# First layer of a four-layer program: side work spread over the steps, heads divided by their sums on VectorE instead of copied by ScalarE

## The chip, the core and the metric

The program runs on one core of a Trainium2 chip. Five engines work side by side on it, each on its own list of instructions in order: TensorE (PE in the profile, with its weight loads as PEld), VectorE (DVE), ScalarE (ACT), GpSimd (POOL) and SyncE (SP), which here only issues DMAs. They wait for each other by semaphores. Matmul results land in eight PSUM banks of 128 x 512 fp32; everything else lies in SBUF. The metric is the device time of the whole program in microseconds, the median of several runs.

## The reference

Four blocks are computed one after the other on x of shape (4, 512, 512), each as x + layernorm(block(layernorm(x))). Only the first two blocks are touched here; the kernel calls them together "the first layer":

```python
x = x + _layernorm(_L0_attn_ref(_layernorm(x), Wq, Wkv, Wo))
x = x + _layernorm(_L0_ffn_ref(_layernorm(x), q_scales, q_vals, bias))
...
# _L0_attn_ref: 32 heads of width 16, one key and one value head for all
q = (h @ Wq).reshape(b, s, 32, 16)
kv = h @ Wkv
k, v = kv[..., :16], kv[..., 16:]
scores = einsum('bqhd,bkd->bhqk', q, k) * 16 ** -0.5
bias = slopes[:, None, None] * (pos[None, None, :] - pos[None, :, None])
scores = where(causal, scores + bias, -inf)
out = einsum('bhqk,bkd->bqhd', softmax(scores), v).reshape(b, s, 512)
return out @ Wo
# _L0_ffn_ref: one product with a dequantized 512 x 512 matrix, plus a bias
```

## The kernel before

The function layer0 holds the first layer. Matmuls are done in fp16 with every operand split in a high and a low part (names ending in _hi and _lo), so one product is three matmuls.

**Steps.** The 32 heads are taken in 16 pairs for each of the 4 batch elements, 64 pairs p in all. The code of every engine is one loop over steps n from -6 to 80, and what an engine does in step n is fixed by lags. In step n:

- TensorE writes five banks of scores of pair n (L598, L600), interleaved with five banks of exponents of pair n-6 (L610, L612), which ScalarE turns into weights (L814, `weights_and_hi`). These are "turns" 0 to 4: one bank of each. After turn 1 comes the product of weights and values of pair n-8 (weigh_values, L628 and L631, 60 small matmuls) into a bank called pv. Its column 16 of every 17 is the sum of the weights.
- VectorE takes the maximum of each scores bank (L976, L978, L981), and subtracts to get the low part of the weights of pair n-7 in two pieces (weights_lo, L990): one ahead of maxima 0 and 1, one ahead of maxima 2 and 3. `mx` and `mp` hold the maxima; every fourth step they are joined (L996, L998).
- GpSimd casts the weights of pair n-6 to fp16 (L533, three casts, the last one for the fifth bank alone) and does the low part of the fifth bank (L535).
- pv of pair n-8: ScalarE copies the bank to the tile `ob` (copy_heads, L821) behind its third exponential. VectorE takes reciprocals of the sums in `ob` into `ro` as nearly the last thing in the step (sum_reciprocals, L1009). GpSimd multiplies one step later (N_LAG = 9, norm_heads, L524) into `on`, named heads_normed in the profile.

**Side work.** The rest of the layer hangs in the same steps, by the tables FRONT, BACK and NORM of due steps, repeated every 16 steps for the next batch element: q (query projection, every fourth step, n = 3, 7, 11, ...), K and V, y (output projection), f (feed-forward), and transposes of rows, four for a batch element: n1 (`front_T`), o (`heads_T`), n2 (`back_T`), n3 (`xT`). others(n) lists the fills of a step. The first of them is done by TensorE around turn 3, the others between turns 3 and 4; a transpose of the maxima, m, comes in steps divisible by 4, ahead of the others but the first. VectorE evacuates the first between maximum 3 and maximum 4 and the others behind maximum 4; ScalarE does the same around its fourth and fifth exponential.

**Banks.** Scores have three banks, exponents two, and all fills of the step besides have three ("rest"), used in turn: pv, first other, m, other others. take(u) makes TensorE wait until the filling three places earlier in that list has been emptied. So a fourth filling in a step waits for the same step's pv bank. Steps with scores that have four or more: 8, 24, 25, 36, 37, 40, 41, 47, 48, 52 and 53. Without scores: 64, 68 and 69.

**Layernorms.** norms_at(n) gives the normalisations due in step n: n1, a1, n2, a2, n3. For n1, n2 and n3 VectorE takes the statistics of four tiles in one step (L907), then the variance (L915, L917); GpSimd computes the reciprocal deviation in the next step (rstd, L510 to L514); at the end of that step ScalarE normalises the four tiles (L807). For a1 and a2 GpSimd then adds the four tiles to `xb` (add_rows, L545), two at the end of one step and two at the start of the next. With scores running, statistics bursts of four stand in steps 3, 19 and 35 (n1), 33 and 49 (n2), 43 and 59 (n3); one more in step 65 (n2). After a K, ScalarE also makes four key stacks at the end of one step (stack_keys, L837).

## Time and profile before

| what | value |
|---|---|
| median of three runs | 2259.62 us (2256.56 to 2260.6) |
| profiled execution | 2258.78 us, span 2256.8 us |
| busy share | PE 92%, DVE 78%, ACT 62%, POOL 41% |
| steps 8 to 69 of the first layer | about 118 to 626 us of the span |
| second layer, from about 710 us | not touched by the change |

The span is the traced part of the execution; about 2 us lie outside. The page's busy shares are averages over stages with different limits. The stage with the change is read by stretches of the span, and within it step by step: a step starts where VectorE takes its first maximum of a pair.

### The profile page before, as it was taken

How to read it: one execution, taken by the hardware profiler on the slowest of the kernel's cores; microseconds unless marked ns; L12 is line 12 of the kernel's file. 1: busy time of each engine (PE TensorE's matmuls, PEld its weight loads, DVE VectorE, ACT ScalarE, POOL GpSimd, SP SyncE). 2: the span in 40 equal slices, each digit the busy share in tenths (PEclk: the TensorE clock that was granted, in tenths of full speed). 3: DMA queues.
4: the chain of work that ended last, by engine and by line, in shares of the span. 5: the costliest groups of instructions: out<-in, count | busy, mean ns of one | idle time of the engine just before them, and what ended most of it. 6: DMA issues, size and time to landing. Idle time of an engine off the chain costs nothing. (4 is left out here: it accounts for less than half of the span.)

```text
span 2256.8 us, 48541 instructions
## 1 busy us (share of the span) xinstructions
PE 2078.5 (92%) x18563; PEld 1258.3 (56%) x18563; DVE 1771.4 (78%) x3711; ACT 1391.5 (62%) x3037; POOL 930.4 (41%) x901
## 2 busy tenths in 40 slices
PE   8688978889767799999999999999999999988998
PEld 3366656566534456666566665656666665533443
DVE  5699898899765787877787887878878787977665
ACT  2555555555644776777777687777777777761222
POOL 0177776678934323233332323333232333353221
PEclk9899989999778999999999999999999999999999
DMA  5210100101022354444444454454344444520100
GB/s 202 78 35 17 44 20 16 46 17 46 3 80 81 71 88 89 90 71 92 85 77 90 81 100 69 81 97 90 68 90 90 71 81 80 101 75 19 38 20 38
DMA packets 390214, 153.81 MB, mean 68 GB/s; under 512 B 358544, under 2 KB 369424, under 8 KB 387936
## 3 DMA queue, kind: packets, MB, share of 16 engines
q1 hardware_dynamic: 389984, 150.71, 30.5%
q8 instruction: 148, 2.42, 0.5%
q14 instruction: 82, 0.67, 0.1%
HBM read 48.69 MB, written 11.53 MB: 27 GB/s over the span
## 5 line engine op out<-in xcount | busy, mean ns | idle before, releaser
L1762 POOL TENSOR_TENSOR q_in_sbuf<-q_in_sbuf,sinq 128x512 f32<-128x512 f32 x128 | 162.6, 1270 | 720.7 <-ACT q_in_sbuf L1894 598.1
L1906 ACT ACTIVATE xp<-xp,nm 128x128 f32<-128x128 f32 (+3 forms) x512 | 281.3, 550 | 199.1 <-DVE nm L1989 199.1
L1788 PE MATMUL bank<-xT_hi,weights_and_hi 128*128 128x512 f16 x1280 | 381.9, 380 | 6.2 <-DVE yacc L2004 3.5
L814 ACT ACTIVATE weights_and_hi<-bank,unit 128x512 f32<-128x512 f32 x320 | 212.0, 687 | 191.4 <-PE bank L612 187.7
L1871 ACT ACTIVATE probs_hi<-xp,rl 128x128 f16<-128x128 f32 (+3 forms) x512 | 245.1, 550 | 67.8 <-DVE rl L2009 64.4
L1958 DVE SCALAR_TENSOR_TENSOR probs_lo<-xp,rl,probs_hi 128x128 f16<-128x128 f32 (+3 forms) x512 | 282.2, 611 | 0.0
L1966 DVE TENSOR_TENSOR q1T_lo<-qf,q1T_hi 128x512 f16<-128x512 f32 x128 | 88.4, 690 | 223.3 <-ACT q1T_hi L1885 223.3
L1989 DVE CUSTOM_DVE_ANT_0 xp<-bank,mask,cs 128x128 f32<-128x128 f32 (+3 forms) x512 | 250.1, 544 | 0.0
L1788 PE MATMUL bank<-xT_lo,weights_and_hi 128*128 128x512 f16 x640 | 243.0, 380 | 0.0
L533 POOL CAST weights_and_hi<-weights_and_hi 128x1024 f16<-128x1024 f32 (+1 forms) x192 | 188.6, 995 | 116.7 <-ACT weights_and_hi L814 116.5
L1788 PE MATMUL bank<-p1T_hi,v_hi 128*128 128x128 f16 x1280 | 223.1, 220 | 3.3 <-DMA p1T_lo<-probs_lo 3.3
L1788 PE MATMUL bank<-p1T_hi,v_lo 128*128 128x128 f16 x1280 | 223.0, 220 | 0.0
L1788 PE MATMUL bank<-p1T_lo,v_hi 128*128 128x128 f16 x1280 | 222.9, 220 | 0.0
L1788 PEld LDWEIGHTS bank<-xT_hi,weights_and_hi 128*128 128x128 f16 x1280 | 124.3, 98 | 159.7 <-issue 13.5
L1769 POOL TENSOR_TENSOR qf<-q_in_sbuf,t 128x512 f32<-128x512 f32 x160 | 203.8, 1274 | 12.7 <-POOL q_in_sbuf L1762 0.2
L1788 PE MATMUL bank<-wo_hi,o1T_hi 128*128 128x512 f16 x512 | 194.8, 380 | 6.3 <-DVE wo_lo L2048 4.7
L1788 PE MATMUL bank<-wo_hi,o1T_lo 128*128 128x512 f16 x512 | 194.7, 380 | 0.0
L1788 PE MATMUL bank<-wo_lo,o1T_hi 128*128 128x512 f16 x512 | 194.6, 380 | 0.0
L598 PE MATMUL bank<-k_stack_max,q_stack 128*128 128x512 f16 (+3 forms) x512 | 139.9, 316 | 51.7 <-DVE mx L976 35.7
L990 DVE TENSOR_TENSOR weights_lo<-weights_and_hi 128x1024 f16<-128x1024 f32 x128 | 180.4, 1414 | 3.9 <-POOL weights_and_hi L533 3.9
L610 PE MATMUL bank<-q_stack,k_stack 128*128 128x512 f16 (+3 forms) x512 | 143.4, 321 | 23.3 <-ACT weights_and_hi L814 20.7
L1788 PE MATMUL bank<-kT_hi,q1T_hi 128*128 128x128 f16 (+3 forms) x512 | 147.0, 300 | 11.0 <-DVE q1T_lo L1966 7.2
(307 smaller groups left out, 5510.5 us busy)
## 6 DMA issues: line engine op xcount, KB each, us to landing
weights_and_hi<-in_wq SPq DMA_DIRECT2D x8, 1024.0 KB, 5.6
raw_o<-in_wo SPq DMA_DIRECT2D x8, 1024.0 KB, 5.8
x_front<-in_x SPq DMA_DIRECT2D x4, 1024.0 KB, 6.6
q_stack<-q_hi SPq DMA_DIRECT2D x64, 64.0 KB, 2.6
xb<-in_x SPq DMA_DIRECT2D x4, 1024.0 KB, 5.5
wup<-in_wup SPq DMA_DIRECT2D x3, 1024.0 KB, 12.1
fused_scratch<-weights_and_hi SPq DMA_DIRECT2D x12, 256.0 KB, 3.0
x_scratch<-xb SPq DMA_DIRECT2D x3, 1024.0 KB, 4.3
```

What stands on the lines that cost most here:

```text
L533: pool.tensor_copy(ph[0][:, p % 2, c0:c1, :], px[:, p % 2, c0:c1, :]).then_inc(s_wh, 1)
L598: pe.matmul(out[:, c:c + w], qs[:, g % GP, pp, t * P:(t + 1) * P], kz[:, g // GP % 2, e, 0:w], start=True, stop=False)
L610: pe.matmul(out[:, c:c + S - j * P], ks[:, g // GP % 2, e, j * P:(j + 1) * P], qs[:, g % GP, pp, j * P:S], start=True, stop=False)
L814: act.activation(px[:, p % 2, i, :], bank_of(("x", p, i))[:, :], ACT.Exp, scale=unit[:, 0:1]).then_inc(s_ed, 1)
L990: dve.tensor_tensor(ph[1][:, p % 2, c, :], px[:, p % 2, c, :], ph[0][:, p % 2, c, :], ALU.subtract).then_inc(s_wl, 1)
L1762: pool.tensor_tensor(qs[:, i % 2, :], qs[:, i % 2, :], rope["sink" if u[0] == "k" else "sinq"][:, :], ALU.mult).then_inc(s_rot, 1)
L1769: pool.tensor_tensor(qf[:, i % 2, :], qs[:, i % 2, :], t2[:, i % 2, :], ALU.add).then_inc(s_qf, 1)
L1788: ins = pe.matmul(out, lhs(a), rhs(c), start=(first and i == 0), stop=(last and i == 2))
L1871: ins = act.activation(pr[0][:, m % 2, c], xp[:, m % 3, c], ACT.Copy, scale=rl[:, m % 3, t:t + 1])
L1906: ins = act.activation(x, x, ACT.Exp, scale=-1.0, bias=nm[:, m % 3, t:t + 1], accum_out=ls[:, m % 3, t:t + 1])
L1958: ins = dve.scalar_tensor_tensor(pr[1][:, m % 2, c], xp[:, m % 3, c], rl[:, m % 3, t:t + 1], pr[0][:, m % 2, c], ALU.mult, ALU.subtract)
L1989: ins = dve.tensor_tensor_reduce(out=xp[:, m % 3, TRI[t]:TRI[t] + w], in0=bank_of(("s", m, i))[:, col:col + w], in1=mask[:, S - w:S], scal ...
```

## The change

**Heads.** copy_heads, the tile `ob` and the semaphore s_pv_out are gone. VectorE takes the reciprocals straight from the pv bank, behind maximum 3 of the same step, then evacuates the first other fill, and then multiplies from the bank into `on`. The multiplication's semaphore, s_heads_normed, now tells TensorE that the pv bank is empty. GpSimd's norm_heads is gone.

**Side work.** The four statistics of n1 go to four steps (the last in the step of the variance, three steps later than before), those of n2 and n3 to two steps, two in each, with the variance one step later. One of a step's statistics stands ahead of the multiplication, the others behind maximum 4. ScalarE normalises two tiles behind its exponentials 3 and 4 of a step, and two behind exponentials 0 and 1 of the next, instead of four at the end. The key stacks are dealt out in the same way, and VectorE's last key operation moves one step later. GpSimd's four additions stand one at the end of a step, one at the start and one at the end of the next, and one at the start of the third. The store of x2 comes one step later.

```diff
-        X_LAG, V_LAG, N_LAG = 6, 8, 9
+        X_LAG, V_LAG = 6, 8
...
-        NORM = {"n1": -13, "a1": 30, "n2": 33, "a2": 40, "n3": 43}
+        NORM = {"n1": -10, "a1": 30, "n2": 34, "a2": 40, "n3": 44}
+        STATS = {"n1": (-13, -12, -11, -10), "n2": (33, 33, 34, 34), "n3": (43, 43, 44, 44)}
...
-        signals = {"s": (s_sf, s_sd), "x": (s_ef, s_ed), "pv": (s_pf, s_pd), ...
+        signals = {"s": (s_sf, s_sd), "x": (s_ef, s_ed), "pv": (s_pf, s_on), ...
...
 # GpSimd
                 for n in STEPS:
-                    for u in norms_at(n - 3):
-                        if u in add_no:
-                            add_rows(u, (2, 3))
+                    adds_at(n - 4, 3)
+                    adds_at(n - 3, 1)
                     for u in norms_at(n - 1):
                         rstd(norm_no[u])
-                    if 0 <= n - N_LAG < NP:
-                        norm_heads(n - N_LAG)
                     if 0 <= n - X_LAG < NP:
                         weights_hi(n - X_LAG)
-                    for u in norms_at(n - 2):
-                        if u in add_no:
-                            add_rows(u, (0, 1))
+                    adds_at(n - 3, 2)
+                    adds_at(n - 2, 0)
...
 # ScalarE
-                        if i == 2 and 0 <= n - V_LAG < NP:
-                            copy_heads(n - V_LAG)
...
-                    b = at(n, FRONT["K"] + 1)
-                    if b is not None:
-                        stack_keys(b)
-                    for u in norms_at(n - 1):
-                        normalise(u)
+                        for u in norms_at(n - 2) if i < 2 else norms_at(n - 1) if i > 2 else ():
+                            normalise(u, i + 2 if i < 2 else i - 3)
+                        if i > 2 and at(n, FRONT["K"] + 1) is not None:
+                            stack_keys(at(n, FRONT["K"] + 1), 0, i - 3)
+                        if i < 2 and at(n, FRONT["K"] + 2) is not None:
+                            stack_keys(at(n, FRONT["K"] + 2), 1, i)
...
 # VectorE
+                def pv_out(p):
+                    return bank_of(("pv", p))[:, 0:2 * TT * EV].rearrange("p (e t c) -> p e t c", e=2, c=EV)
+
                 def sum_reciprocals(p):
-                    dve.wait_ge(*emptied[("pv", p)])
-                    if p >= 3:
-                        dve.wait_ge(s_on, p - 2)
-                    dve.reciprocal(ro[:, p % 3, :, :], ob[:, p % 3, :, :, E0]).then_inc(s_ro, 1)
+                    dve.wait_ge(*filled[("pv", p)])
+                    dve.reciprocal(ro[:, p % 2, :, :], pv_out(p)[:, :, :, E0]).then_inc(s_ro, 1)
+
+                def norm_heads(p):
+                    b, c = p // PAIRS, 2 * (p % PAIRS) * E0
+                    if p % GP == 0 and b >= 1:
+                        dve.wait_ge(*filled[("o", b - 1, p % PAIRS // GP)])
+                    dve.wait_ge(s_ro, p + 1)
+                    o = pv_out(p)
+                    dve.tensor_tensor(on[:, :, c:c + 2 * E0].rearrange("p t (e c) -> p e t c", e=2),
+                                      o[:, :, :, 0:E0], ro[:, p % 2, :, :].unsqueeze(3).to_broadcast([P, 2, TT, E0]),
+                                      ALU.mult).then_inc(s_on, 1)
...
                     if 0 <= n < NP:
                         maximise(n, (2, 3))
+                    if 0 <= n - V_LAG < NP:
+                        sum_reciprocals(n - V_LAG)
                     for u in extra[:1]:
                         evacuate(u)
+                    if at(n, FRONT["K"] + 1) is not None:
+                        add_key_maxima(at(n, FRONT["K"] + 1))
+                    some_statistics(stats_at(n)[:1])
+                    if 0 <= n - V_LAG < NP:
+                        norm_heads(n - V_LAG)
                     if 0 <= n < NP:
                         maximise(n, (4,))
...
                     for u in extra[1:]:
                         evacuate(u)
+                    some_statistics(stats_at(n)[1:])
                     for u in norms_at(n):
-                        kind, b = u
...
                         variance(u)
-                    if 0 <= n - V_LAG < NP:
-                        sum_reciprocals(n - V_LAG)
```

VectorE around step 19, whose n1 statistics are dealt out. First the kernel before:

```order
L978 TENSOR_REDUCE mp<-bank 128x4 x2
L953 SCALAR_TENSOR_TENSOR q_lo<-bank,fq,q_hi 128x512
L981 TENSOR_REDUCE mx<-bank 128x2
L907 BN_STATS st<-x_front 128x6 x4
L915 BN_AGGR mv<-st 128x2 x4
L917 TENSOR_SCALAR ve<-mv 128x4
L1009 RECIPROCAL ro<-ob 128x8
L996 TENSOR_REDUCE mx<-mp 128x8
L998 COPY mx<-mp 128x8
L990 TENSOR_TENSOR weights_lo<-weights_and_hi 128x1024
```

The same place in the change, down to the second statistics in step 20:

```order
L964 TENSOR_REDUCE mp<-bank 128x4 x2
L996 RECIPROCAL ro<-bank 128x8
L939 SCALAR_TENSOR_TENSOR q_lo<-bank,fq,q_hi 128x512
L891 BN_STATS st<-x_front 128x6
L1004 TENSOR_TENSOR heads_normed<-bank,ro 128x2x4x16
L967 TENSOR_REDUCE mx<-bank 128x2
L982 TENSOR_REDUCE mx<-mp 128x8
L984 COPY mx<-mp 128x8
L976 TENSOR_TENSOR weights_lo<-weights_and_hi 128x1024
L962 TENSOR_REDUCE mx<-bank 128x1 x2
L976 TENSOR_TENSOR weights_lo<-weights_and_hi 128x1024
L964 TENSOR_REDUCE mp<-bank 128x4 x2
```

One statistics instruction and the multiplication stand where four statistics and the variance did; the reciprocal has gone up, from the end of the step to behind maximum 3.

VectorE in step 24, which has two transposes besides m. First before:

```order
L990 TENSOR_TENSOR weights_lo<-weights_and_hi 128x1024
L978 TENSOR_REDUCE mp<-bank 128x4 x2
L921 TENSOR_TENSOR front_T_lo<-bank,front_T_hi 128x4x128
L981 TENSOR_REDUCE mx<-bank 128x2
L1002 SCALAR_TENSOR_TENSOR m_lo<-bank,m_hi 32x128
L921 TENSOR_TENSOR front_T_lo<-bank,front_T_hi 128x4x128
L1009 RECIPROCAL ro<-ob 128x8
L990 TENSOR_TENSOR weights_lo<-weights_and_hi 128x1024
```

And in the change:

```order
L976 TENSOR_TENSOR weights_lo<-weights_and_hi 128x1024
L964 TENSOR_REDUCE mp<-bank 128x4 x2
L996 RECIPROCAL ro<-bank 128x8
L905 TENSOR_TENSOR front_T_lo<-bank,front_T_hi 128x4x128
L1004 TENSOR_TENSOR heads_normed<-bank,ro 128x2x4x16
L967 TENSOR_REDUCE mx<-bank 128x2
L988 SCALAR_TENSOR_TENSOR m_lo<-bank,m_hi 32x128
L905 TENSOR_TENSOR front_T_lo<-bank,front_T_hi 128x4x128
L976 TENSOR_TENSOR weights_lo<-weights_and_hi 128x1024
```

The bank of pv is now emptied by L1004, behind maximum 3 and the first transpose's low part.

TensorE in step 24, between turns 3 and 4, with its waits. First before:

```order
L639 MATMUL bank<-ident,mx 128x128 [waits s_maxima,s_queries_out]
L645 MATMUL bank<-ident,x_front 128x128 [waits s_pv_out,s_rows_normed]
L645 MATMUL bank<-ident,x_front 128x128 x3
L598 MATMUL bank<-k_stack_max,q_stack 128x256 [waits s_scores_maximised]
L600 MATMUL bank<-tri,far 128x128
```

And in the change:

```order
L633 MATMUL bank<-ident,mx 128x128 [waits s_maxima,s_queries_out]
L639 MATMUL bank<-ident,x_front 128x128 [waits s_heads_normed,s_rows_normed]
L639 MATMUL bank<-ident,x_front 128x128 x3
L592 MATMUL bank<-k_stack_max,q_stack 128x256 [waits s_scores_maximised]
L594 MATMUL bank<-tri,far 128x128
```

TensorE's list is the same; its second transpose of the step waits for VectorE's multiplication where it waited for ScalarE's copy.

## Rows read from the trace of the kernel before

**Rows 1.** The page: busy time of each engine.

```profile
PE 2078.5 (92%) x18563; PEld 1258.3 (56%) x18563; DVE 1771.4 (78%) x3711; ACT 1391.5 (62%) x3037; POOL 930.4 (41%) x901
```

**Rows 2.** Stretches: length, busy us (instructions) by engine, granted clock, DMA share, GB/s.

```profile
118.00:626.00 508.00, 439.12 (x6413) 306.85 (x6414) 451.54 (x703) 294.61 (x523) 381.80 (x366) 0.93 0.08 27
183.50:189.70 6.20, 4.97 (x94) 3.71 (x93) 6.20 (x10) 3.51 (x6) 5.08 (x6) 1.00 0.18 58
196.00:206.10 10.10, 7.55 (x108) 4.97 (x105) 9.27 (x22) 5.01 (x9) 5.40 (x7) 0.98 0.01 2
224.80:232.90 8.10, 8.07 (x113) 5.47 (x110) 7.43 (x13) 4.45 (x8) 7.32 (x7) 1.00 0.01 3
252.80:264.00 11.20, 11.17 (x135) 6.96 (x132) 7.50 (x13) 4.96 (x9) 7.30 (x7) 1.00 0.01 4
304.30:315.80 11.50, 6.49 (x126) 4.97 (x122) 10.29 (x18) 4.16 (x8) 11.34 (x11) 0.96 0.12 37
395.00:409.00 14.00, 12.14 (x140) 7.22 (x136) 11.03 (x23) 5.52 (x10) 12.26 (x12) 1.00 0.21 76
585.20:626.00 40.80, 32.20 (x500) 22.76 (x497) 31.12 (x36) 22.28 (x40) 37.88 (x34) 0.72 0.01 2
```

**Rows 3.** Waits from 118 to 626 us: who for whom, us, times, longest.

```profile
PE bank L598 <- DVE mx L976: 32.3, 21, 4.8
PE bank L610 <- ACT weights_and_hi L814: 20.7, 21, 3.2
```

**Rows 4.** Timeline of VectorE near 302 us: start, length, instruction.

```profile
302.08 0.23 DVE L948 TENSOR_TENSOR v<-bank,v 128x64 f16<-128x64 f32 x1 [0.29 <-ACT v L782]
302.23 0.68 DVE L981 TENSOR_REDUCE mx<-bank 128x2 f32<-128x512 f32 x1
```

**Rows 5.** Timeline of VectorE at the end of step 17.

```profile
187.59 0.19 DVE L1009 RECIPROCAL ro<-ob 128x8 f32<-128x8 f32 x1
187.70 2.04 DVE L990 TENSOR_TENSOR weights_lo<-weights_and_hi 128x1024 f16<-128x1024 f32 x1
```

**Rows 6.** Timeline of GpSimd at the same time.

```profile
187.50 1.16 POOL L535 TENSOR_TENSOR weights_lo<-weights_and_hi 128x512 f16<-128x512 f32 x1
188.62 1.39 POOL L524 TENSOR_TENSOR heads_normed<-ob,ro 128x128 f32<-128x128 f32 x1
```

**Rows 7.** VectorE, groups by form from 118 to 626 us: count, busy, mean ns.

```profile
L990 DVE TENSOR_TENSOR weights_lo<-weights_and_hi 128x1024 f16<-128x1024 f32 x125 | 175.6, 1409 | 3.9 <-POOL weights_and_hi L533 3.9
```

**Rows 8.** The same by its tile: count, shortest, median and longest ns.

```profile
L990 DVE TENSOR_TENSOR weights_lo<-weights_and_hi x125: 1165/1211/2311, 119.1 to 623.6; 128x1024 f16<-128x1024 f32 x125
```

**Rows 9.** Timeline of TensorE in step 24, behind turn 3.

```profile
234.35 0.60 PE L645 MATMUL bank<-ident,x_front 128*128 128x128 f32 x4
234.78 0.27 PE L598 MATMUL bank<-k_stack_max,q_stack 128*128 128x256 f16 x1
```

**Rows 10.** Timeline of VectorE in step 24.

```profile
235.16 1.27 DVE L978 TENSOR_REDUCE mp<-bank 128x4 f32<-128x512 f32 x2
236.36 0.67 DVE L921 TENSOR_TENSOR front_T_lo<-bank,front_T_hi 128x512 f16<-128x512 f32 x1
236.96 0.68 DVE L981 TENSOR_REDUCE mx<-bank 128x2 f32<-128x512 f32 x1
```

**Rows 11.** Timeline of VectorE in step 19.

```profile
201.49 2.46 DVE L907 BATCH_NORM_STATS2 st<-x_front 128x6 f32<-128x512 f32 x4
204.06 0.38 DVE L915 BATCH_NORM_AGGREGATE mv<-st 128x2 f32<-128x6 f32 x4
```

**Rows 12.** ScalarE, groups by form from 118 to 626 us.

```profile
L821 ACT ACTIVATE ob<-bank 128x136 f32<-128x136 f32 x63 | 17.4, 276 | 0.0
```

**Rows 13.** Timeline of VectorE: low part of the queries in steps 23 and 47.

```profile
229.15 0.75 DVE L953 SCALAR_TENSOR_TENSOR q_lo<-bank,fq,q_hi 128x512 f16<-128x512 f32 x1 [0.63 <-ACT q_hi L790]
...
443.33 0.75 DVE L953 SCALAR_TENSOR_TENSOR q_lo<-bank,fq,q_hi 128x512 f16<-128x512 f32 x1 [2.02 <-ACT q_hi L790]
```

**Rows 14.** GpSimd, groups by form from 585.2 to 626 us.

```profile
L524 POOL TENSOR_TENSOR heads_normed<-ob,ro 128x128 f32<-128x128 f32 x6 | 4.2, 708 | 0.1
```

More of the change, by code:

```diff
@@ L407, in norms_at, with stats_at @@
             return out
+        def stats_at(n):
+            return [(kind, b, t) for kind in STATS for t in range(TT)
+                    for b in (at(n, STATS[kind][t]),) if b is not None and has(kind, b)]
         norms = [u for n in STEPS for u in norms_at(n)]
@@ L482, in _ @@
                         stack_queries(g)
-                    b = at(n, NORM["a2"] + 3)
+                    b = at(n, NORM["a2"] + 4)
                     if b is not None and b < LAST:
@@ L805, in normalise @@
                         act.wait_ge(s_ad, TT * (add_no["a" + str(int(kind[1]) - 1), b] + 1))
-                    for t in range(TT):
-                        act.activation(dst[:, t, :], src[:, t, :], ACT.Identity, scale=rs[:, t:t + 1],
-                                       bias=nb[:, t:t + 1]).then_inc(s_nm, 1)
+                    act.activation(dst[:, t, :], src[:, t, :], ACT.Identity, scale=rs[:, t:t + 1],
+                                   bias=nb[:, t:t + 1]).then_inc(s_nm, 1)
                 def exponential(p, i):
@@ L829, in maxima_hi, with stack_keys @@
                                    scale=-1.0 / MAXU).then_inc(s_mh, 1)
-                def stack_keys(b):
-                    for i, k in enumerate((kz, ks)):
-                        act.wait_ge(s_kb, 2 * b + i + 1)
-                        if b >= 2:
-                            act.wait_ge(*filled[("x", PAIRS * (b - 1) - 1, 4)])
-                        for e, half in enumerate(("even", "odd")):
-                            act.activation(k[:, b % 2, e, :], kb[:, i, :], ACT.Copy,
-                                           scale=row[half][:, 0:1]).then_inc(s_kr, 1)
+                def stack_keys(b, i, e):
+                    k, half = (kz, ks)[i], ("even", "odd")[e]
+                    act.wait_ge(s_kb, 2 * b + i + 1)
+                    if b >= 2:
+                        act.wait_ge(*filled[("x", PAIRS * (b - 1) - 1, 4)])
+                    act.activation(k[:, b % 2, e, :], kb[:, i, :], ACT.Copy,
+                                   scale=row[half][:, 0:1]).then_inc(s_kr, 1)
                 for n in STEPS:
@@ L936, in join_keys, with add_key_maxima @@
                                              ALU.mult, ALU.add).then_inc(s_kb, 1)
+                def add_key_maxima(b):
                     dve.wait_ge(s_kb, 2 * b + 1)
@@ L1031, in _ @@
                         evacuate(u)
+                    some_statistics(stats_at(n)[1:])
                     for u in norms_at(n):
-                        kind, b = u
-                        if kind == "n1":
-                            dve.wait_ge(s_xf, 16 * b)
-                        for t in range(TT):
-                            if kind == "n1":
-                                statistics(t, xf)
-                            elif kind in ("n2", "n3"):
-                                dve.wait_ge(s_ad, TT * add_no["a" + str(int(kind[1]) - 1), b] + t + 1)
-                                statistics(t, xb)
                         variance(u)
-                    if 0 <= n - V_LAG < NP:
-                        sum_reciprocals(n - V_LAG)
                     if n == NP + V_LAG + 2:
```

37 lines of the change are left out of this document (15 added, 22 removed).

## The prediction

> **What bounds the kernel now.** I read the page first, for the shares of the whole program [rows 1], then the stretches of the first layer, then single steps. TensorE's 92% of the page says little here: the change lies between 118 and 626 us, and in that stretch VectorE is busy 451.5 of 508 us, TensorE 439.1, GpSimd 381.8 and ScalarE 294.6 [rows 2]. VectorE and TensorE are so close that each step decides for itself. Step 17 is an ordinary one, with nothing on the side: 6.2 us, VectorE busy for all of it, TensorE for 4.97. Step 23 has a q fill: 8.1 us, TensorE busy for 8.07, VectorE for 7.43. Step 27 with q and y is TensorE's alone: 11.2 us against VectorE's 7.5. TensorE can't run far ahead, since the scores have three banks for five fills a step, and can't catch up later what it lost. So a step costs about the larger of the two engines' loads in it, plus what they spend waiting for each other. In the waits of the stretch TensorE stands 32.3 us for VectorE's maxima and 20.7 us for ScalarE's exponentials [rows 3]: the first come behind bursts of VectorE's side work, the second behind bursts of ScalarE's. These two are what dealing out can win. The time before and after the stretch has no instruction that changes much, and I take it as it is.
>
> **1. The multiplication on VectorE.** 64 instructions of 128 x 128 out of PSUM are added. No row has this form. A 128 x 64 one of the same kind holds VectorE for 0.15 us (302.08 to 302.23) [rows 4]; a 128 x 512 one for 0.60 us (236.36 to 236.96) [rows 10]. Between them, by elements, lies 0.15 + 64/448 x 0.45 = 0.21 us; that is an estimate, and 0.15 and 0.60 are its bounds. I take 0.2, near the smaller, since 128 elements are 64 from the one and 384 from the other. The reciprocal held the engine for only 0.11 us though it lasts 0.19 [rows 5]; the multiplication needs its result, so in steps without a fill between the two another 0.1 us is lost. Together some 0.3 us a step, 19 us over 64 steps (at the bounds 15 and 45). But not all of it moves the end. At the end of step 17 VectorE's weights_lo starts at 187.70 and takes 2.04 us, where the shortest takes 1.165 [rows 8], and GpSimd's L535 of 187.50 to 188.66 explains it: VectorE got on when GpSimd was through [rows 5, 6]. What delays VectorE by 0.3 us there only shortens this hold. L990 means 1409 ns over 125 instructions [rows 7], 0.24 above the shortest [rows 8], so the holds sum to 0.24 x 125 = 30 us; I find the first piece, or the small copy ahead of it, held by over 0.2 us in 36 of the 64 steps. Of the 28 others eight have the bank wait of point 2, which counts its own 0.3. That leaves 20 x 0.3 = **+6 us**. That the new instruction is held itself by GpSimd I exclude: the low parts that read a bank, like L921, take 0.67 us each time [rows 10].
>
> **2. The pv bank comes free late.** ScalarE emptied it behind its third exponential; now VectorE does, behind maximum 3 and the evacuation of the first fill. In steps with four fills TensorE needs that very bank for the fourth. In step 24 it did so at 234.35 [rows 9]. VectorE finishes maximum 3 about 236.36 and the first low part at 236.96 [rows 10]; with reciprocal and multiplication it is 237.3. TensorE stands for 3 us with turn 4 queued behind the transposes. Then four transposes (0.43 us to the next matmul [rows 9], and the scores' bank 0.35 us after that) fill the bank for maximum 4 at about 238.2, which VectorE could have taken at 237.3: 1 us idle, and maximum 4 comes 1.2 us later than before. ScalarE's fifth exponential and, behind it, the high part of the second transpose come later too, for which VectorE then waits a second time, 0.9 us; and GpSimd's L535, released by that exponential, now meets weights_lo, 0.5 us. Sum 2.6 us for step 24. Steps 8, 36 and 52 have the same pattern: 4 x 2.6 = 10. In steps 25 and 41 the fourth fill is the last: 2 x 2.2 = 4. In steps 37, 40, 47, 48 and 53 TensorE comes late by itself, with a projection or V ahead, and I take 1 us each, for the part that VectorE still needs from its evacuation to the multiplication: 5. Together **+19 us**; from both sides 5 (if only the wait for maximum 4 counts and half of it is made good in the next step) to 40 (if each costs 3.5).
>
> **3. Statistics dealt out.** Step 19 (q and a burst) takes 10.1 us where step 23 (q) takes 8.1; step 33 takes 11.5 where an ordinary one takes 6.2; step 43 (q, y) 14.0 where step 27 takes 11.2 [rows 2]: bursts cost 2.0, 5.3 and 2.8 us, 3.4 in the mean. VectorE's own work in one is 4 x 0.6 + 0.4 + 0.2 = 3.0 us [rows 11], and it stays. So a full step's filling gains only 0.4 us a burst; it was not the size of the burst but VectorE's load that was paid. To that comes that single statistics in ordinary steps go partly into the holds of point 1, I take 1.2 us a burst. Eight bursts: 8 x 1.6 = **-13 us**; between -3 and -25, the latter if all 3.0 are hidden. TensorE's idle time behind a burst isn't a gain by itself: VectorE was working.
>
> **4. ScalarE.** The 64 copies of 276 ns [rows 12] lay in time when it waited for TensorE: 0 by themselves, as ScalarE has 3.51 us of work in a 6.2 us step [rows 2]. The bursts of four normalisations and four key stacks are another matter: exponentials 0 and 1 of the next step come late, TensorE waits for them (20.7 us [rows 3]), and VectorE then waits in the q step behind, 2.02 us in step 47 against 0.63 in step 23 [rows 13]. Two of four now stand ahead of exponential 4 or behind it, where they delay the cast and L535. I count half: **-10 us**, between 0 and -20. What is late next is exponential 4.
>
> **5. GpSimd.** Its multiplication goes. In ordinary steps it lay behind weights_lo and ahead of a cast that had time (188.62) [rows 6]: 0. From 585.2 on GpSimd is busy 37.9 of 40.8 us [rows 2], and there the six that go take 4.2 us [rows 14]: **-4 us**. But GpSimd no longer waits there for VectorE's reciprocal, and in its place a cast of the next pair can start just ahead of weights_lo, which is then held as in [rows 5]. By when exponential 1, L535 and weights_lo come in each step, 14 steps are exposed, to 0.5 to 0.76 us; half of it is **+4 us**. The Trainium skill (SBUF — State Buffer, section Who interferes with whom) says that a VectorE instruction with two SBUF inputs and a GpSimd instruction that reads SBUF exclude each other, and whoever starts first keeps the ports for its whole length; the trace's 2.04 us agrees, and by that rule the full 8 to 11 us are paid, the third rival below.
>
> The queues: on SP only the store of x2 moves, by one step, and the load of the next xb behind it waits for a later normalisation, two steps ahead of its first use. Cost 0; if it were late, GpSimd's additions would wait.
>
> **Sum:** 6 + 19 - 13 - 10 - 4 + 4 = +2 us against the profiled execution of 2258.8 us; with rounding of the terms, and since the median of the runs is 0.8 us above that execution, I say 2262 us.
>
> **The rivals.**
> - *The bank wait is hidden and the spreading works.* TensorE has 1.2 us of slack in an ordinary step, and VectorE's delays might be swallowed by the holds. Then point 2 is 5, the others as above, or point 3 at -20: 6 + 5 - 16 - 12 - 4 + 4 = -17, 2243 us. For it: the 30 us of holds. Against: the fourth fill and turn 4 stand in one queue. Chance 0.32.
> - *The bank wait weighs double (the slower side).* The granted clock was 0.93 in the mean of the stretch and 0.72 from 585.2 on, where TensorE is busy for 32.2 of 40.8 us [rows 2]: where it stands more, the chip grants less. Eleven new stalls of 3 us can bring more of the lower level, 1.2 GHz, and a step with one costs 3.5 us instead of 1 to 2.6 where TensorE is needed. From 30 us for the eleven steps on it decides: 6 + 36 - 13 - 10 - 4 + 4 = +19, 2279 us. Chance 0.2.
> - *GpSimd's cast gets ahead of VectorE in all exposed steps*: 8 to 11 us instead of 4, and in the steps of point 2 as well: +9, 2269 us. Chance 0.1.
> - *It doesn't deal out as it says*: no. The order of instructions shows each move.
>
> **How the numbers follow.** The sum as it stands, 2262 us with 2256 to 2268, has 0.38, of which 0.25 lie within 0.2% of before (4.5 us, about what a measurement can tell) and 0.13 above. Faster by over 0.2%: 0.32 from the first rival. Slower: 0.13 + 0.2 + 0.1 = 0.43. The range from 2238 to 2282 leaves out a tenth at either side.
>
> **What would show it.** In the trace of the changed kernel: L1004 near 280 ns, 64 times, and weights_lo's mean below or above 1409 ns (point 1 or the third rival). In step 24 TensorE idle for about 3 us ahead of the transpose L639, released by heads_normed, and VectorE idle ahead of maximum 4 (point 2): a sum of waits of TensorE for heads_normed near 20 to 30 us; under 10 would be the first rival. VectorE's waits for q_hi near 0.65 each (point 4). TensorE's waits for ScalarE down from 20.7 us by half. The clock in the stretch at 0.93 or above, against 0.90 or lower for the second rival. The whole is wrong if the stretch of 508 us moves by over 20 us either way.

## The result and the profile after

The changed kernel takes 2284.6 us (median, 2278.3 to 2287.5) against 2259.7 for the kernel before: a ratio of 1.0109, with a 95% interval of 1.0086 to 1.0132. It is slower by about 25 us. The forecast was 2262 us, with a range up to 2282. Slower was the likeliest of the three outcomes, at 0.43, but the size lies outside the range.

The page of the kernel after: the span and the busy times, to be laid beside [rows 1].

```profile
span 2282.9 us, 48332 instructions
...
PE 2082.5 (91%) x18563; PEld 1259.4 (55%) x18563; DVE 1787.6 (78%) x3775; ACT 1378.9 (60%) x2973; POOL 890.6 (39%) x837
```

VectorE has gained 16 us of work, ScalarE and GpSimd have lost 13 and 40, TensorE has gained 4, and the span is 26 us longer: 6.5 us ahead of step 8, 16.6 in steps 8 to 69, the rest behind. No engine's load says that. The waits from 118 to 650 us do (who waited for whom: us, times, longest), beside [rows 3]:

```profile
PE bank L639 <- DVE heads_normed L1004: 31.3, 13, 3.5
...
DVE mx L967 <- PE bank L594: 22.7, 15, 2.8
PE bank L604 <- ACT weights_and_hi L807: 20.4, 17, 7.2
PE bank L592 <- DVE mx L962: 17.0, 19, 2.5
...
DVE q_lo L939 <- ACT q_hi L784: 2.0, 4, 0.6
```

The first row didn't exist before: TensorE waits 31.3 us, in 13 places, for VectorE's multiplication, which now frees the pv bank. The second is the answer to it: VectorE waits 22.7 us for maximum 4's bank, where the kernel before had 7.9 us. Against them stands what the dealing out won: TensorE's wait for maxima of L962 is 17.0 us, from 32.3, and VectorE's for q_hi 2.0, from 11.5 over the whole stretch.

Step by step, from VectorE's first maximum of a pair to the next, in us, from one trace of each kernel. The last row ends where VectorE starts the first weights_lo of step 70. The last four columns are experiments told below.

| step | before | after | late release only | dealing out only, early start-up | after, early start-up | after, early release |
|---|---|---|---|---|---|---|
| 7 | 7.6 | 13.3 | 7.6 | 6.6 | 6.6 | 7.5 |
| 8 (n1, m, n1) | 6.7 | 11.5 | 10.5 | 7.5 | 10.5 | 8.6 |
| 17 (ordinary) | 6.2 | 6.2 | 6.2 | 6.2 | 6.2 | 6.2 |
| 19 (q, n1 due) | 10.1 | 8.0 | 10.1 | 8.0 | 8.0 | 8.1 |
| 24 (n1, m, n1) | 6.7 | 11.4 | 10.5 | 7.4 | 10.5 | 8.8 |
| 25 (n1, n1, o) | 7.1 | 9.6 | 10.5 | 7.1 | 9.6 | 8.0 |
| 33 and 34 (n2 due) | 17.7 | 17.3 | 18.7 | 17.6 | 17.3 | 17.5 |
| 45 (K) | 12.4 | 9.5 | 12.1 | 8.8 | 9.5 | 9.5 |
| 52 (n2, m, n2) | 6.7 | 11.0 | 10.5 | 6.7 | 11.4 | 8.8 |
| 8 to 69 | 504.6 | 521.2 | 540.5 | 480.6 | 517.5 | 498.8 |

Three things are in it: steps with four fills, of which nine of eleven grew, by 2 to 5 us (47 shrank and 48 hardly moved); steps with a due layernorm or behind one, most of which shrank; and step 7, which the prediction never looked at.

### The profile page after: what moved, and what is told of

Read it like the earlier page. It is cut to its first block and busy times, and to the rows that moved or that the text cites. A ratio compares the mean times of both kernels' runs of the same rounds, so it can differ in the third digit from the quotient of the medians.

```text
span 2282.9 us, 48332 instructions
## 1 busy us (share of the span) xinstructions
PE 2082.5 (91%) x18563; PEld 1259.4 (55%) x18563; DVE 1787.6 (78%) x3775; ACT 1378.9 (60%) x2973; POOL 890.6 (39%) x837
## 5 line engine op out<-in xcount | busy, mean ns | idle before, releaser
L526 POOL CAST weights_and_hi<-weights_and_hi 128x1024 f16<-128x1024 f32 (+1 forms) x192 | 194.5, 1025 | 202.5 <-ACT weights_and_hi L807 191.2
L1791 PEld LDWEIGHTS bank<-xT_hi,weights_and_hi 128*128 128x128 f16 x1280 | 124.4, 98 | 159.8 <-issue 12.9
L976 DVE TENSOR_TENSOR weights_lo<-weights_and_hi 128x1024 f16<-128x1024 f32 x128 | 187.7, 1470 | 8.0 <-POOL weights_and_hi L526 8.0
L604 PE MATMUL bank<-q_stack,k_stack 128*128 128x512 f16 (+3 forms) x512 | 144.8, 324 | 22.1 <-ACT weights_and_hi L807 20.4
## 6 DMA issues: line engine op xcount, KB each, us to landing
wup<-in_wup SPq DMA_DIRECT2D x3, 1024.0 KB, 12.1
```

The source lines that it names most:

```text
L526: pool.tensor_copy(ph[0][:, p % 2, c0:c1, :], px[:, p % 2, c0:c1, :]).then_inc(s_wh, 1)
L604: pe.matmul(out[:, c:c + S - j * P], ks[:, g // GP % 2, e, j * P:(j + 1) * P], qs[:, g % GP, pp, j * P:S], start=True, stop=False)
L976: dve.tensor_tensor(ph[1][:, p % 2, c, :], px[:, p % 2, c, :], ph[0][:, p % 2, c, :], ALU.subtract).then_inc(s_wl, 1)
L1791: ins = pe.matmul(out, lhs(a), rhs(c), start=(first and i == 0), stop=(last and i == 2))
```

## Step 24 in the trace after

VectorE's timeline (start, length, instruction, and in brackets the idle time before it and who ended it):

```profile
245.22 0.19 DVE L996 RECIPROCAL ro<-bank 128x8 f32<-128x8 f32 x1
245.34 0.63 DVE L905 TENSOR_TENSOR front_T_lo<-bank,front_T_hi 128x512 f16<-128x512 f32 x1
245.90 0.27 DVE L1004 TENSOR_TENSOR heads_normed<-bank,ro 128x128 f32<-128x128 f32 x1
248.15 0.69 DVE L967 TENSOR_REDUCE mx<-bank 128x2 f32<-128x512 f32 x1 [1.98 <-PE bank L594]
248.75 0.27 DVE L988 SCALAR_TENSOR_TENSOR m_lo<-bank,m_hi 32x128 f16<-32x128 f32 x1
249.99 0.69 DVE L905 TENSOR_TENSOR front_T_lo<-bank,front_T_hi 128x512 f16<-128x512 f32 x1 [0.96 <-ACT front_T_hi L760]
250.59 1.87 DVE L976 TENSOR_TENSOR weights_lo<-weights_and_hi 128x1024 f16<-128x1024 f32 x1
```

TensorE's in the same step:

```profile
246.31 1.09 PE L639 MATMUL bank<-ident,x_front 128*128 128x128 f32 x4 [3.26 <-DVE heads_normed L1004]
247.19 0.42 PE L592 MATMUL bank<-k_stack_max,q_stack 128*128 128x256 f16 x1
```

The two fences are point 2 of the prediction, link by link. TensorE stands 3.26 us (the prediction: 3), VectorE then 1.98 us for maximum 4 (1.0) and 0.96 us for the second transpose (0.9), and weights_lo takes 1.87 us, held for 0.7 by GpSimd (0.5). What was too small is the second link, and the rows of the stretch say why (length, then busy us and instructions of the engines, granted clock). They are the step, the part of it behind the stall, and the step behind:

```profile
241.10:252.50 11.40, 8.14 (x107) 6.22 (x104) 8.46 (x13) 5.63 (x11) 5.03 (x6) 0.70 0.01 3
246.30:252.40 6.10, 6.08 (x82) 4.62 (x82) 3.29 (x5) 2.44 (x4) 1.77 (x2) 0.53 0.03 5
252.50:262.10 9.60, 7.17 (x115) 5.65 (x113) 7.56 (x13) 4.93 (x9) 4.56 (x5) 1.00 0.13 43
```

The clock was 0.70 in the step and 0.53 behind the stall: there TensorE worked mostly at the lower of its two levels, 1.2 GHz instead of 2.4. From the transposes to the next matmul it took 0.88 us (246.31 to 247.19), where [rows 9] had 0.43. I had priced the recovery at the full clock.

Step 41 of the changed kernel shows what the clock alone is worth. Below stand that step and the same one with an early GpSimd instruction (an experiment told below). TensorE stands 2.61 us for the multiplication in both, but the granted clock is 0.84 in the one and 1.00 in the other, and the step takes 10.5 and 9.6 us: 0.9 us.

```profile
397.30:407.80 10.50, 7.77 (x105) 5.80 (x103) 7.57 (x13) 6.15 (x11) 6.12 (x7) 0.84 0.11 38
389.00:398.60 9.60, 6.22 (x102) 4.76 (x103) 7.55 (x13) 5.56 (x11) 6.09 (x7) 1.00 0.12 41
```

## Step 7: GpSimd starts up in front of everybody

GpSimd's timeline in the kernel after, from 60 us on:

```profile
106.44 1.04 POOL L526 CAST weights_and_hi<-weights_and_hi 128x1024 f16<-128x1024 f32 x1 [39.85 <-ACT weights_and_hi L807]
109.00 2.66 POOL L526 CAST weights_and_hi<-weights_and_hi 128x1024 f16<-128x1024 f32 x2 [1.52 <-ACT weights_and_hi L807]
118.61 1.14 POOL L528 TENSOR_TENSOR weights_lo<-weights_and_hi 128x512 f16<-128x512 f32 x1 [6.96 <-issue]
119.73 1.05 POOL L515 TENSOR_TENSOR rs<-ve,mhalf 128x4 f32<-128x4 f32 x1
```

and in the kernel before:

```profile
66.42 0.13 POOL L504 MEMSET v<- 128x8 f16 x1
97.92 1.06 POOL L510 TENSOR_TENSOR rs<-ve,mhalf 128x4 f32<-128x4 f32 x1 [31.37 <-DVE ve L917]
```

"<-issue" means that GpSimd waited for nothing that the profile shows. Its last instructions before the layer are reductions over partitions, then memsets. In both kernels the trace has a configuration record of GpSimd at the first tensor_tensor behind them: before, at 66.6 us, under the 31 us in which GpSimd waited for the first variance; after, at 111.7 us, since the variance came three steps later and the first tensor_tensor was now L528, which pair 0's product needs. The 7 us stood under VectorE's next weights_lo, which waited 5.66 us:

```profile
122.47 2.03 DVE L976 TENSOR_TENSOR weights_lo<-weights_and_hi 128x1024 f16<-128x1024 f32 x1 [5.66 <-POOL weights_and_hi L526]
```

The Trainium skill (GPSIMD Engine Reference, section 2.1 Instruction dispatch) says that the first call to freshly loaded GpSimd code pays a load of some 6 us, for which the profile has no instruction. The trace agrees, with 6.96 us.

## Experiments

Every kernel was timed in rounds against the kernel before; ratios are given, since the baseline moved by a few us between the batches (2261.9, 2258.1 and 2258.6 us).

**The late release alone.** Nothing is dealt out, nobody has more work: VectorE's reciprocal of the copy moves to the place of the multiplication, and frees the bank.

```diff
-        signals = {... "pv": (s_pf, s_pd), ...
+        signals = {... "pv": (s_pf, s_ro), ...
...
                     for u in extra[:1]:
                         evacuate(u)
+                    if 0 <= n - V_LAG < NP:
+                        sum_reciprocals(n - V_LAG)
...
-                    if 0 <= n - V_LAG < NP:
-                        sum_reciprocals(n - V_LAG)
```

> The kernel before with one thing moved: VectorE's reciprocal (still out of ScalarE's copy) stands where the change has its multiplication, and its semaphore, not the copy's, tells TensorE that the pv bank is empty. ScalarE's copy and GpSimd's multiplication stay; nothing is dealt out; VectorE has no work more. My theory (the late release of the pv bank costs most of the 25 us): 18 to 28 us over the kernel before, 2278 to 2288 us, with TensorE idle for about 3 us in step 24 ahead of the second transpose. Rival one (VectorE's added instructions cost it, 0.3 us a step): within 3 us of the kernel before. Rival two (the dealt-out side work costs it): the same, within 3 us.

Measured: 2297.8 us, ratio 1.0161 (1.0142 to 1.0181), 36 us over before. More than the whole change, and above the 18 to 28 expected. Its waits:

```profile
PE bank L645 <- DVE ro L1009: 25.9, 12, 3.3
DVE mx L981 <- PE bank L600: 25.0, 15, 2.8
```

Steps 8, 24 and 52 take 10.5 us where they took 6.7, and the clock in the stretch falls to 0.90 from 0.93. TensorE's stall, the second link and the third are 2.78, 1.98 and 0.96 us in its step 24, nearly those of the changed kernel. VectorE's extra work isn't needed for the loss.

**The heads' part alone.** The kernel before with the change's reciprocal and multiplication out of the bank, without copy and without GpSimd's multiplication.

```diff
-                        if i == 2 and 0 <= n - V_LAG < NP:
-                            copy_heads(n - V_LAG)
...
+                    if 0 <= n - V_LAG < NP:
+                        sum_reciprocals(n - V_LAG)
                     for u in extra[:1]:
                         evacuate(u)
+                    if 0 <= n - V_LAG < NP:
+                        norm_heads(n - V_LAG)
```

> The kernel before with the heads' part of the change alone: no copy, reciprocal and multiplication by VectorE out of the bank; the side work is where it was. My theory: 20 to 30 us over before, 2280 to 2290, little more than the late release alone. Rival one (VectorE's 64 multiplications): about 19 us over before here, and nothing for the late release alone. Rival two (the dealing out): at most 5 us over before.

Measured: 2295.7 us, ratio 1.0149 (1.0128 to 1.017). It is over the 2280 to 2290 expected, and the same as the late release alone within the intervals. As long as the side work isn't dealt out, the 64 multiplications on VectorE, less what ScalarE and GpSimd are spared, cost nothing that can be measured; the two intervals together leave room for some 4 us.

**The dealing out alone.** The change with the old path of the heads.

```diff
+                        if i == 2 and 0 <= n - V_LAG < NP:
+                            copy_heads(n - V_LAG)
...
+                    if 0 <= n - N_LAG < NP:
+                        norm_heads(n - N_LAG)
```

> The kernel of the change with the old path of the heads: ScalarE copies pv, GpSimd multiplies, reciprocal at the end of the step. All the dealing out of side work stays. My theory: the dealing out gains 8 to 15 us, and the first tensor instruction of GpSimd now meets 7 us of its own start-up in step 7, so together 2 to 9 us under before, 2251 to 2258. Rival two (the dealing out costs): 10 us or more over before, 2270 and up.

Measured: 2242.7 us, ratio 0.9918 (0.99 to 0.9936), 19 us under before, and step 7 takes 13.4 us here too. The dealing out is a gain, larger than the 2 to 9 us that I wrote.

**The start-up out of the way.** The changed kernel with one instruction ahead of the memsets:

```diff
+        warm = sc.sb("warm", [P, TT])
...
+                pool.tensor_tensor(warm[:, :], C["mhalf"][:, 0:TT], C["mhalf"][:, 0:TT], ALU.mult)
                 pool.memset(mx[:, :, :], 0.0)
```

> The changed kernel with one instruction added: a GpSimd tensor_tensor of 128 x 4 into a tile of its own at the start of the first layer, when GpSimd is idle. My theory (the 7.0 us that GpSimd stands in step 7 of the changed kernel, ahead of its first tensor_tensor of the layer, is a one-time start that the kernel before had while idle): 5 to 6.5 us less than the changed kernel, 2278 to 2280 us, and step 7 back at about 7.6 us from 13.3. Rival (the gap is a wait for data, or hidden by other waits of step 7): no change, 2284 us.

Measured: 2278.8 us, ratio 1.0084 (1.0062 to 1.0106). The medians differ by 5.8 us, as expected, but these two intervals overlap; what shows the mechanism is the trace. GpSimd's rows from 60 us:

```profile
72.97 0.19 POOL L507 TENSOR_TENSOR warm<-mhalf 128x4 f32<-128x4 f32 x1 [41.92 <-issue]
...
107.60 1.04 POOL L528 CAST weights_and_hi<-weights_and_hi 128x1024 f16<-128x1024 f32 x1 [33.93 <-ACT weights_and_hi L809]
109.72 1.59 POOL L528 CAST weights_and_hi<-weights_and_hi 128x1024 f16<-128x1024 f32 x2 [1.08 <-ACT weights_and_hi L809]
111.39 2.08 POOL L530 TENSOR_TENSOR weights_lo<-weights_and_hi 128x512 f16<-128x512 f32 x1
```

The start-up now ends at 72.97, while nobody needs GpSimd, and L530 follows the cast at once. Step 7 takes 6.6 us instead of 13.3, and step 8 starts at 119.0 us of the span instead of 124.4.

**Both gains together.** The dealing out with the old path of the heads and the early GpSimd instruction.

> The dealing out with the old path of the heads, and with one GpSimd tensor_tensor of 128 x 4 at the start of the first layer. Theory: the two effects add, 2242.7 minus 5.8 us = about 2237 us, step 7 near 7 us. Rival (in this kernel other waits of step 7 take the place of the start-up): 2242 us.

Measured: 2234.9 us, ratio 0.99 (0.9886 to 0.9915): some 23 us under the kernel before, near the 2237 us expected. Against the dealing out alone that is 4 us by the ratios, again with intervals that overlap; step 7 is 6.6 us from 13.4. This is the fastest kernel of the study.

**What is in the dealing out.** First ScalarE's part alone, in the kernel before (the key stacks are dealt out in the same way, not shown):

```diff
...
-                    for u in norms_at(n - 1):
-                        normalise(u)
+                        for u in norms_at(n - 2) if i < 2 else norms_at(n - 1) if i > 2 else ():
+                            normalise(u, i + 2 if i < 2 else i - 3)
```

> The kernel before with ScalarE's part of the dealing alone: normalisations and key stacks two and two around the exponentials; statistics, additions and heads as before. The prediction took 10 us for this part (bounds 0 and 20): 2250 us. If the statistics are the whole gain, it stays at 2260; if ScalarE's bursts are, it comes to 2240.

Measured: 2242.4 us, ratio 0.9931 (0.9916 to 0.9946): 16 us. TensorE's wait for the exponentials falls from 20.7 to 14.0 us, of which 8.5 are a single wait near 586 us, and VectorE's for q_hi from 11.5 to 7.7.

Then everything but ScalarE's part, with the early GpSimd instruction (the same lines the other way round, in the kernel of the last paragraph but one):

> The dealing out of VectorE's statistics and key maxima and of GpSimd's additions, without ScalarE's: normalisations and key stacks in bursts at the end of a step as before; old path of the heads; with the early GpSimd instruction, so that its start-up doesn't enter. The prediction took 13 us for this part (bounds 3 and 25): 2247 us. If it and the ScalarE part add, their two gains make the 23 to 25 us of both together.

Measured: 2252.6 us, ratio 0.9974 (0.9964 to 0.9983): 6 us, where 13 had been forecast. The two make 22 of the 23 us. With ScalarE's part alone step 31 (q, behind a1's variance) is 6.6 us from 8.7 and step 47 8.6 from 11.7; dealing the statistics makes step 33 8.5 from 11.6, and step 34 9.1 from 6.1. There VectorE's work has only moved. At the burst of step 19 it has not: that step is 8.0 from 10.1, and steps 20 to 22 together only 0.6 longer.

**Earlier release.** The changed kernel with the early GpSimd instruction, reciprocal and multiplication behind the second piece of weights_lo:

```diff
                         weights_lo(n - X_LAG - 1, 1)
+                    if 0 <= n - V_LAG < NP:
+                        sum_reciprocals(n - V_LAG)
+                    if 0 <= n - V_LAG < NP:
+                        norm_heads(n - V_LAG)
                     if 0 <= n < NP:
                         maximise(n, (2, 3))
-                    if 0 <= n - V_LAG < NP:
-                        sum_reciprocals(n - V_LAG)
...
-                    if 0 <= n - V_LAG < NP:
-                        norm_heads(n - V_LAG)
```

> The changed kernel with the early GpSimd instruction, and with VectorE's reciprocal and multiplication ahead of maxima 2 and 3, behind the second piece of weights_lo, instead of behind maximum 3 and the first fill's evacuation. The work is the same, only the pv bank comes free some 2 us earlier, while VectorE still has maxima 2 and 3 to take. Theory (the place of the release costs it): TensorE's wait for the multiplication falls from 31 us to under 10, steps 8, 24, 36 and 52 to about 7 us from 11, and the time to 2243 to 2252 us. Rival (any multiplication on VectorE that frees the bank costs as much, by its work and by the casts that now get ahead of weights_lo): 2270 us or more.

Measured: 2253.2 us, ratio 0.9979 (0.997 to 0.9989), against 1.0084 with the late place: 24 us for moving two instructions within a step. The waits:

```profile
PE bank L641 <- DVE heads_normed L1006: 10.9, 7, 2.3
...
DVE mx L969 <- PE bank L596: 5.7, 5, 1.5
```

The place of the release is what cost. The first wait is slightly over the bound of 10 that I had set, the time slightly over its range; step 24 takes 8.8 us, not 7.

**The late release where the side work is dealt out.**

> The dealing out with the old path of the heads and the early GpSimd instruction (2234.9 us), and in it the late release alone: the reciprocal out of ScalarE's copy stands where the change has its multiplication and frees the bank. If the late release costs here what it cost in the kernel before (36 us), 2271 us; then the changed kernel with the early GpSimd instruction (2278.8) has 8 us of other cost from VectorE's multiplication and GpSimd's casts. If it costs 44 us here, 2279, the multiplication is free and the wait weighs more where the side work is dealt out.

Measured: 2267.6 us, ratio 1.0039 (1.0026 to 1.0051), 0.0139 over the kernel without it, or 31 us; it was 36 in the kernel before. The wait doesn't weigh more here. So 0.0045 remain between this and the changed kernel with the early instruction (1.0084), 10 us for VectorE's multiplication and the casts; the two intervals make that 4 to 16 us.

This kernel also shows point 2's links at the full clock. Step 24 of it, and below it step 24 of the kernel before with the late release alone:

```profile
235.20:244.80 9.60, 7.12 (x121) 5.71 (x118) 7.74 (x13) 5.92 (x13) 7.21 (x7) 1.00 0.02 4
238.10:248.60 10.50, 7.10 (x100) 5.42 (x98) 7.56 (x12) 4.33 (x9) 5.11 (x6) 0.84 0.02 3
```

With 1.00 granted TensorE stands 2.46 us, and VectorE waits 1.21 us for maximum 4 and 0.65 us for the second transpose: near the 1.0 and 0.9 of the prediction. With 0.84 they are 2.78, 1.98 and 0.96 us. The lower level doesn't follow each stall: steps 24 and 52 of this kernel kept 1.00, steps 8 and 36 had 0.84 and 0.85.

**The multiplication without the release.** VectorE multiplies, but out of ScalarE's copy, which frees the bank.

```diff
-                    o = pv_out(p)
+                    o = ob[:, p % 3, :, :, :]
                     dve.tensor_tensor(on[:, :, c:c + 2 * E0].rearrange("p t (e c) -> p e t c", e=2),
-                                      o[:, :, :, 0:E0], ro[:, p % 2, :, :].unsqueeze(3).to_broadcast([P, 2, TT, E0]),
+                                      o[:, :, :, 0:E0], ro[:, p % 3, :, :].unsqueeze(3).to_broadcast([P, 2, TT, E0]),
                                       ALU.mult).then_inc(s_on, 1)
```

> The same kernel (2234.9 us) with GpSimd's multiplication taken over by VectorE, but out of ScalarE's copy in SBUF, which frees the bank as before; the reciprocal behind maximum 3, the multiplication where the change has it. Only VectorE's work and GpSimd's relief change. The prediction's points 1 and 5 took 6 and 4 us for the two costs and 4 us for the gain: 2241 us. If VectorE's 64 multiplications cost their full 0.3 us each, 2254 us; if the holds swallow them, 2235.

Measured: 2248.5 us, ratio 0.9955 (0.994 to 0.997), 12 us over the kernel with GpSimd's multiplication, where 6 were forecast and 19 would have been the full price. Its rows, by form from 110 to 660 us (count, busy us, mean ns), and the one of the changed kernel, which reads the bank:

```profile
L989 DVE TENSOR_TENSOR weights_lo<-weights_and_hi 128x1024 f16<-128x1024 f32 x128 | 182.2, 1428 | 3.1 <-POOL weights_and_hi L530 2.8 <-issue 0.3
...
L1016 DVE TENSOR_TENSOR heads_normed<-ob,ro 128x128 f32<-128x128 f32 x64 | 28.1, 439 | 0.2
```

```profile
L976 DVE TENSOR_TENSOR weights_lo<-weights_and_hi 128x1024 f16<-128x1024 f32 x128 | 187.7, 1470 | 8.0 <-POOL weights_and_hi L526 8.0
...
L1004 DVE TENSOR_TENSOR heads_normed<-bank,ro 128x128 f32<-128x128 f32 x64 | 17.8, 277 | 0.2
```

The mean of 439 ns hides two kinds. By the tile's row (shortest, median and longest ns) most of the 64 take what they take out of the bank, whose longest is 292 ns:

```profile
L1016 DVE TENSOR_TENSOR heads_normed<-ob,ro x64: 266/285/1247, 125.1 to 619.5; 128x128 f32<-128x128 f32 x64
```

21 of the 64 took 415 to 1247 ns, and each of these ended 0.14 or 0.15 us behind the end of a GpSimd instruction. Step 21, VectorE's multiplication and GpSimd's instruction:

```profile
217.77 1.25 DVE L1016 TENSOR_TENSOR heads_normed<-ob,ro 128x128 f32<-128x128 f32 x1
217.59 1.28 POOL L532 TENSOR_TENSOR weights_lo<-weights_and_hi 128x512 f16<-128x512 f32 x1
```

So out of the copy the multiplication is held by GpSimd in a third of the steps, and out of the bank in none: that never took over 292 ns. The holds make 10 us over the 64, so this kernel overstates the price by up to that, and the experiment is no clean measure of point 1. Step by step, ordinary steps 10, 12, 16 and 17 stay at 6.2 us; steps 18, 20 and 21 go from 6.3 and 6.2 to 7.1 or 7.2, and in each of the three the multiplication was held for about 0.9 us. In the changed kernel, which reads the bank, steps 20 and 21 take 6.3 and 6.2 us.

**The earliest release.** One place further ahead, between maximum 1 and the second piece of weights_lo.

> The changed kernel with the early GpSimd instruction and with reciprocal and multiplication one place further ahead than in the last such run: between maximum 1 and the second piece of weights_lo, 1.2 us earlier. There TensorE still waited 10.9 us for the multiplication at 2253 us. If what was left of the cost is that wait, it falls below 3 us and the time to about 2245 us; if it is VectorE's work and GpSimd's casts, it stays at 2250 to 2254. What could turn against it: VectorE now waits for the product itself in steps where TensorE is behind.

Measured: 2254.2 us, ratio 0.9981 (0.9972 to 0.999), at the upper end of the second case that I had named; no further gain, though TensorE's wait is nearly gone. Two rows from its waits:

```profile
PE bank L594 <- DVE mp L966: 31.0, 29, 2.1
...
PE bank L594 <- DVE mx L964: 22.2, 26, 2.3
```

and what waited for the multiplication (from the instructions that read heads_normed or its bank):

```profile
  PE bank L641: 1.9, 5
```

What is left of the cost, 18 us over the fastest kernel, isn't the bank wait. TensorE now waits for VectorE's maxima, 53.2 us in the two rows where the fastest kernel has 36.7 (22.7 and 14.0), so VectorE's load and holds are a likely seat. A part can be seen in the steps: ordinary ones (10, 12, 16, 17) take 6.5 or 6.6 us here, 6.2 in the kernel before, the changed one and the fastest. How the rest splits between the multiplication, the reciprocal's wait and GpSimd's casts stays open.

## Why the prediction was wrong

By ratios, the change is made of: late release +31 (over the fastest kernel), dealing out -23, start-up +6, multiplication and the relief of GpSimd +10. Sum +24, measured +25. These four are the differences along one chain of kernels, from the one before to the changed one, so that they add up is no check of them. My sum was 19 - 23 + 0 + 6 = +2. Two steps of it failed: the pv bank's term was too small by 12 to 17 us, and the start-up stood at nothing.

1. **The multiplication on VectorE (+6, with point 5's 4 and -4 also +6).** Its price was right: 275 ns in the median and 277 in the mean against 280, and at 191.67 and 191.88 of the trace after the next instruction follows by 0.21 us. That holds swallow it in ordinary steps was right: 6.2 us in the kernel before and in the changed one. Steps with a single dealt-out statistics cost no more either: 20 and 21 take 6.3 and 6.2 us with the change and 6.2 with the dealing out alone. Measured +10 in the dealt-out kernel (4 to 16), and between -9 and +4 in the other: the term isn't refuted. Between the late release in the dealt-out kernel and the changed kernel with the early instruction, steps 15, 32, 42, 48 and 52 grew most, by 1 to 1.9 us each, and a few others shrank; why these is open.
2. **The pv bank (+19; measured +31 to +36).** The mechanism, its steps and its three links are as written; the term is the one mis-sized. In the kernel with the late release alone it is 36 us. The eleven steps that I priced at 19 cost 30: steps 8, 24, 36 and 52 cost 3.8, 3.8, 3.2 and 3.8 instead of 2.6, steps 25 and 41 3.4 and 2.9 instead of 2.2, and the five where TensorE is late by itself 3.2, 1.2, 1.5, 1.2 and 1.9 instead of 1. Another 5 us lie behind step 63, mostly in steps 64 and 69: they have four fills but no scores, and my term left them out without a reason. A part of the excess is the lower clock behind the stall. In six of the eleven steps (8, 24, 25, 37, 41 and 52) the granted clock was 0.68 to 0.87 where the kernel before had 1.00; at the 0.9 us of step 41 above that is 5 of the 17 us, an estimate. It stood as the second rival, with the bound of 30 us from which it decides and 2279 us as its time; I gave it 0.2, although the trace of before already has 0.52 granted in a step at 315.8 us (its row stands below the list), and 0.72 in the tail. Its sign in the prediction, a clock of 0.90 in the stretch, didn't show in the changed kernel: steps 8 to 69 have 0.93, as before. Two effects lie over each other there. The dealing out alone, with the early instruction, has 0.97, and the late release takes it to 0.94; in the kernel before it took 0.93 to 0.90.
3. **Statistics dealt out (-13; measured -6).** Nearer to what the first half of that paragraph said, that VectorE's work stays, than to the holds I added.
4. **ScalarE (-10; measured -16).** I took half of TensorE's 20.7 us. With ScalarE's part alone that wait is 14.0 us, a third less; the changed kernel has 20.4, of which 7.2 are the start-up in step 7 and 6.4 one wait near 628 us. VectorE's waits for q_hi fell from 11.5 to 7.7 us with this part alone, and to 2.0 in the changed kernel, and that comes on top. Points 3 and 4 together are right, -23 against -22 to -23, by errors that cancel: that is luck.
5. **GpSimd.** weights_lo's mean rose from 1414 to 1470 ns, 7 us over 128 instructions: near the 8 to 11 of the third rival and not the 4 of the sum. It takes both parts of the change: with the heads' part alone the mean is 1395 ns, with the dealing out alone 1398.
6. **Not in the sum: the start-up (+6).** By the dealing out without and with the early instruction it is +4. Both differences lie within the noise of the times; the 7 us in step 7 stand in the traces of all kernels that have the variance late and no early instruction (the changed one and the dealing out alone). "The time before and after the stretch has no instruction that changes much" is the second step that failed. The change moves n1's first variance behind the first exponentials, so I had its order of instructions in hand, and [rows 2] began at 118 us; the 31 us in which GpSimd had seemed merely idle had hidden the start-up.

The row of the kernel before that point 2 speaks of, behind a step of 6.80 us in which TensorE was busy for 2.68 (columns as above):

```profile
315.80:322.00 6.20, 5.47 (x54) 3.79 (x55) 6.20 (x11) 3.81 (x6) 6.03 (x8) 0.52 0.00 0
```

The first rival (the wait hidden, 0.32) is refuted by the late release alone, and by the 31.3 us of waits in the changed kernel, for which the prediction had 20 to 30 and under 10 as the rival's sign. "It doesn't deal out as it says" needed no run.

## What to carry to other kernels

When an operation moves from one engine to another, ask first which semaphore it carried: here the copy's early release was worth 31 to 36 us, while the new place of the multiplication decides more (24 us) than its work. List every step that has the wait, those of the tail too, before pricing it. A stall put into TensorE's list can cost the clock behind it as well: 0.9 us in step 41, with the same stall. And before moving the first instruction of a kind on GpSimd behind others, look whether it stood under a long idle time: a one-line instruction in idle time keeps its start-up off the path.

## What the runs showed that I had not expected

- Changing from reductions over partitions to tensor_tensor costs GpSimd 6.96 us once in this layer, with no busy instruction in the profile; it starts when the instruction comes up, even if that then waits for a semaphore (66.6 us in the kernel before), but casts and memsets ahead of it don't start it.
- The same 128 x 128 multiplication with a broadcast operand takes 260 to 292 ns out of PSUM every time. Out of SBUF its median is 285 ns, but 21 of 64 wait for a GpSimd instruction to end and take up to 1247 ns.
- Dealing ScalarE's bursts of four over two steps brings 16 us, though the engine is busy for only 62% of the span.
- In the second layer of the kernel before GpSimd changes between reductions and tensor_tensor 16 times. It stands ahead of L1762 for 122.6 us in all that the profile puts down to "issue"; whether that lies on the path no run here tests.
